# Block attention in a two-layer gated kernel: a subtraction and a score product take other places in two queues, and GpSimd takes over two small jobs

## The chip, the cores and the metric

The kernel runs on one core of one Trainium2 chip. The metric is the device time of one execution in microseconds; before the change the median of three runs is 186.9 (186.82 to 187.08). Lower is better.

## What is computed

Eight blocks of 128 rows by 256 features pass through two layers. Each layer adds a gated mixing of the context and a gated feed-forward part to its input. The change touches the second layer's attention, whose core is:

```python
q = _qdq(layernorm(x)) @ _qdq(wq).T + bq            # 16 heads of 16, int8-like rounding of inputs and weights
k, v = split(ctx @ wkv.T + bkv)
attn = softmax(q @ k.T / 4)                          # per block and head, 128 x 128
o = attn @ v
x = x + tanh(g) * (_qdq(o) @ _qdq(wp).T + bp)
def _qdq(x):
    s = max(max(abs(x), axis=-1) / 127, 1e-8)
    return clip(round(x / s), -127, 127) * s
```

Before it stand a long convolution with a router-gated low-rank product, behind it a mixture of eight experts.

## The kernel before

The kernel is written by hand, one queue per engine; the order of the instructions in each queue is the order in which the Python code issues them, and semaphores tie the queues together. Blocks are pipelined: in step s of the attention loop (s from 0 to 7) the engines work on several blocks at once. The input rounding and the query product are for block s + 2 or s + 3, the scores for block s + 1, maximum and subtraction for block s, turning, exponentials and values for block s - 1, and the output's normalisation, rounding and projection for blocks s - 2 and s - 3.

One block's way through a step, with the lines of the kernel before:

- Scores: `a_scores` (PE, L1657) multiplies 16 heads into PSUM banks 0 to 3. It overwrites the scores of the block before, so it waits for all subtractions of that block.
- Maximum: `a_max` (DVE, L1156), two halves of eight heads, written negated.
- Subtraction: `a_subtract` (DVE, L1166) for heads 0 to 11 in two instructions, and `a_last_subtract` (ACT, L781), four instructions, for heads 12 to 15.
- Turning: `a_turn(b, k)` (PE, L1671), four transposes each, k from 0 to 3, into PSUM banks 4 and 5 in turn. Turn 3 needs ACT's subtractions; each turn needs that the exponential two before it has emptied its bank.
- Exponential: `a_exp(b, k)` (ACT, L786), one for each turn.
- Values: `a_values` (PE, L1687), heads 0 to 3 and 8 to 11 after exponential 1, the others after exponential 3. Then `o_pe_` (ACT, L792) empties the bank and `o_rows` (PE, L1696) turns the result back.
- Output: `o_norm` (DVE, L1176 to L1187) has five parts: reciprocal of the sums, product, largest magnitude, scale, reciprocal of the scale. `o_round` (GpSimd, L546) rounds, `o_transpose` (PE, L1714), `o_ev_` (ACT, L811), `o_project` (PE, L1720), `o_y_` (ACT, L806), and on GpSimd `finish` (L552, L554).
- Next queries: normalised rows (`rows` on GpSimd, L535 and L538, from block 4 on), their scale (`a_quant` on DVE, L1143 to L1147), rounding `a_zq_` (ACT, L754), `a_transpose` (PE, L1618), `a_zt_` (ACT, L759), `a_project` (PE, L1624), `a_q0_` (ACT, L765), `a_q_transpose` (PE, L1631), `a_q_` (ACT, L771).

GpSimd's other work in the loop is the masked key blocks (`block_keys`, L525), `bias_rows` (L530) and, from its iteration 7 on, the normalisation's root for the experts (`late_rstd`, L559 and L561, a power). The semaphore `o_n` counts the parts of `o_norm`; `a_z` those of `a_quant`; `a_zq` and `o_qp` the rounded blocks.

Of the kernel before, what the change touches and what calls it, by code (L numbers as in the profile page):

```python
# [28 lines left out]
P = 128  # L29
# [48 lines left out]
def build(nc, x, ctxr, kern, consts, rows, cols, wff, bt, wkv, wqp, gate, w1, w3, w2, sw1, sw3, sw2, out):  # L78
    with ExitStack() as ctx:
# [3 lines left out]
        def sem(name):  # L83
            return ctx.enter_context(nc.semaphore(name))
# [28 lines left out]
        LNV = sb("LNV", [P, NB])  # L113
        EPSC = sb("EPSC", [P, 1])
        HALFM = sb("HALFM", [P, 1])
        WS = sb("WS", [P, 4])
        WR = sb("WR", [P, 4])
        SWPB = sb("SWPB", [P, DM])
# [184 lines left out]
        o_sc = sem("o_sc")  # L303
        a_zp = sem("a_zp")
        o_qp = sem("o_qp")
        y_d, x3_d = sem("y_d"), sem("x3_d")

        m_ln, m_rs, m_z, m_tr, m_zt, m_gl, m_ge, m_gt = (sem(n) for n in (
# [28 lines left out]
        WARM = 26  # L337
        FRT = 8
        AZT = 4
        ONT = 5  # L340
        LATE = 3
        MGT = 2 * GT + 4

# [76 lines left out]
        def sums(g, n):  # L420

            return PS[:, ((0, 1), (7, 6))[g][n], :]

        def expert(v):

            return v - v // (NE + 1) - 1
# [55 lines left out]
        @block.gpsimd  # L482
        def _(pool):
            nc.gpsimd.memset(ONES[:, :], 1.0).then_inc(ones_s, 1)
            nc.gpsimd.memset(HALFM[:, :], -0.5).then_inc(ones_s, 1)
            nc.gpsimd.memset(EPSC[:, :], EPS).then_inc(ones_s, 1)
            nc.gpsimd.memset(GL[:, :, :], FULL).then_inc(ones_s, 1)
# [44 lines left out]
            def rows(b):  # L532

                pool.wait_ge(a_rs, 2 * (b + 1))
                nc.gpsimd.tensor_scalar(NMR[:, b:b + 1], MV[:, b, 0:1], -1.0, None, ALU.mult).then_inc(a_zp, 1)  # L535
                pool.wait_ge(a_zq, b - 1)
                pool.wait_ge(a_zp, 2 * (b - GT) + 1)
                nc.gpsimd.tensor_scalar(AZ[:, b % 2, :], X[:, b, :], NMR[:, b:b + 1], RS[:, b:b + 1],  # L538
                                        ALU.add, ALU.mult).then_inc(a_zp, 1)

            def o_round(b):

                pool.wait_ge(o_n, ONT * (b + 1))
                if b >= 2:
                    pool.wait_ge(o_tr, b - 1)
                nc.gpsimd.tensor_scalar(OT_[:, b % 2, :], O[:, b % 2, :], OR[:, b:b + 1], ROUND_H,  # L546
                                        ALU.mult, ALU.add).then_inc(o_qp, 1)
# [71 lines left out]
            for b in range(2, NB):  # L619
                block_keys(b)  # L620
                if b == NB - 1:
                    late_rstd(0)
                if 3 <= b < NB - 1:
                    rows(b + 1)
                if b >= 6:
                    finish(b - 6)
                bias_rows(b)
                if b >= 4:
                    o_round(b - 4)
            for b in (1, 2):  # L630
                late_rstd(b)
                finish(b + 1)
                o_round(b + 3)
# [14 lines left out]
        def _(act):  # L648
# [99 lines left out]
                rstd(a_ln, 2 * (b + 1), b, b + 1, a_rs, 2 * b)  # L748

            def a_zq_(b):  # L750
                act.wait_ge(a_z, AZT * (b + 1) - max(0, b + 1 - GT))
                if b >= 2:
                    act.wait_ge(a_tr, b - 1)
                nc.scalar.activation(AT_[:, b % 2, :], AZ[:, b % 2, :], ACT.Copy, bias=ROUND_H, scale=AR[:, b:b + 1]  # L754
                                     ).then_inc(a_zq, 1)
# [36 lines left out]
                nc.scalar.copy(OTS[:, b % 2, :], PS[:, 7, :]).then_inc(o_pe, 1)  # L792

            def o_q_(b):
                act.wait_ge(o_n, ONT * (b + 1))
                if b >= 2:
                    act.wait_ge(o_tr, b - 1)
                nc.scalar.activation(OT_[:, b % 2, :], O[:, b % 2, :], ACT.Copy, bias=ROUND_H, scale=OR[:, b:b + 1]
                                     ).then_inc(o_q, 1)
# [67 lines left out]
            for s in range(NB):  # L867
                if s + 2 < NB:
                    a_zt_(s + 2)
                if s == 0:  # L870
                    a_last_subtract(0)
                    values_out(NB - 2)
                if s >= 1:
                    a_exp(s - 1, 0)
                if s + 2 < NB:
                    a_q0_(s + 2)
                if s >= 1:
                    a_exp(s - 1, 1)
                if s >= 1:
                    a_last_subtract(s)  # L880
                if s + 2 < NB:
                    a_q_(s + 2)
                if 1 <= s < NB - 4:
                    a_rstd(s + 4)
                if s >= 1:
                    a_exp(s - 1, 2)
                    a_exp(s - 1, 3)
                if s >= 3:
                    o_ev_(s - 3)
                if s + 3 < NB:  # L890
                    a_zq_(s + 3)
                if s == NB - 1:
                    m_rstd(NB - 5)
                if s >= 3:
                    o_y_(s - 3)
                if s >= 1:
                    o_pe_(s - 1)
                if s >= 5:
                    m_zt_(s - 5)
# [60 lines left out]
        def _(dve):  # L960
# [323 lines left out]
            for s in range(NB):  # L1284
                norm, new, moe, ahead = s >= 2, s + 3 < NB, s >= 4, 1 <= s < NB - 4
                if s >= 1:
                    a_max(s, 0)
                    a_max(s, 1)
                    a_subtract(s, 0)
                a_subtract(s, 1)  # L1290
                if s == 0:
                    f_out(NB - 1)
                if ahead:
                    a_stats(s + 4, 0)
                if norm:
                    o_norm(s - 2, 0)
                if ahead:
                    a_stats(s + 4, 1)
                if norm:
                    o_norm(s - 2, 1)  # L1300
                if norm:
                    o_norm(s - 2, 2)
                if s >= 5:
                    m_rows(s - 5)
                if norm:
                    o_norm(s - 2, 3)
                if new:
                    a_quant(s + 3, 0)
                if norm:
                    o_norm(s - 2, 4)  # L1310
                if new:
                    a_quant(s + 3, 1)
                if new:
                    a_quant(s + 3, 2)
                if moe:
                    m_stats(s - 4, 0)
                if new:
                    a_quant(s + 3, 3)
                if moe:
                    m_stats(s - 4, 1)  # L1320
# [113 lines left out]
        def _(pe):  # L1434
# [176 lines left out]


            def a_transpose(b):
                pe.wait_ge(a_zq, b + 1)
                chain_free(b - 2)
                for k in range(NL):
                    at = 64 * k
                    ins = TR(PS[:, a_bank(b), at:at + 64].bitcast(F16), ATH[:, b % 2, P * k:P * k + P, 0], IDH[:, :])  # L1618
                ins.then_inc(a_tr, 1)
# [58 lines left out]
            def a_values(b, k):  # L1678

                if b >= 1 and k == 0:  # L1680
                    pe.wait_ge(o_n, ONT * (b - 1) + 2)
                elif k == 0:
                    pe.wait_ge(x2, NB)
                pe.wait_ge(a_ex, 4 * b + 2 * (k % 2) + 2)
                pe.wait_ge(v_b, b + 1)
                for n in range(4):
                    ins = M(PS[VW * n:VW * n + VW, 7, P * k:P * k + P], V[:, b, 4 * k + n, :],  # L1687
                            ET[:, b % 2, place(4 * k + n), :], start=True, stop=True)
                if k == 3:
                    ins.then_inc(a_pv, 1)  # L1690
# [97 lines left out]
            for s in range(NB):  # L1788
# [16 lines left out]
                    a_q_transpose(s + 2)  # L1805
                if s >= 1:
                    a_turn(s - 1, 2)
                    a_turn(s - 1, 3)
                if s >= 1 and s + 1 < NB:
                    a_scores(s + 1)  # L1810
                if s == NB - 1:
                    m_logits(0, 0, 2)
                if s >= 3:
# [47 lines left out]
            def e_out(v):  # L1861
                g, e = divmod(v, NE + 1)
                if v < UNITS - 1:
                    pe.wait_ge(e_ht, v + 1)
                if v == 0:
                    pe.wait_ge(y_d, LATE)
                elif e == 0:
                    pe.wait_ge(o_n, ONT * (NB - 1) + 2)
                    pe.wait_ge(m_ge, NG)
                for j in range(GT):  # L1870
                    if v == UNITS - 1 and j % 2 == 0:
                        pe.wait_ge(last_ht, j // 2 + 1)
                    src = HT[:, v % 2, :] if e >= 1 else HST

                    ins = M(acc(g, j), src[:, P * j:P * j + P],  # L1875
                            W2[:, e - 1, :] if e >= 1 else SW2, start=(e == 0 and j % 2 == 0),
                            stop=(e == NE), skip_group_check=True)
                    if v == UNITS - 1 and j % 2 == 1:
                        ins.then_inc(last_acc, 1)
                if v < UNITS - 1:  # L1880
                    ins.then_inc(e_acc, 1)
# [91 lines left out]
```

## Time and profile before

| | |
|---|---|
| median of three runs | 186.9 us |
| profiled execution | 186.96 us, span 185.0 us |
| TensorE clock granted | 0.997 of full speed |
| busy over the span | PE 169.5, PEld 115.7, DVE 151.6, ACT 111.2, GpSimd 102.7 us |
| ahead of step 1 of the attention loop | 92.8 us |
| steps 1 to 7 | 47.0 us: PE 41.0, DVE 43.2, ACT 42.1, GpSimd 25.3 us busy |
| the rest | 45.2 us |

The span is the time from the first to the last instruction of the profiled execution; the time of that execution is 1.96 us longer. PE is TensorE's matmul, PEld its weight load, DVE VectorE, ACT ScalarE, POOL GpSimd. A busy time is a union of intervals, so overlapping instructions of one engine count once. A name such as L786 is a line of the kernel.

### The profile page before, as it was taken

To read this page: it belongs to the slowest core of one execution; us is meant where nothing else is said; L and a number is where in the kernel's file an instruction comes from. 1 tells how busy PE (TensorE), PEld (TensorE's weight loads), DVE (VectorE), ACT (ScalarE), POOL (GpSimd) and SP (SyncE) were. 2 spreads that over 40 slices of the span, in tenths; PEclk is the share of its full clock that TensorE was granted. 3 is DMA by queue.
4 is the path that set the end of the run, shared out by engine and by line. 5 is a ranking of instruction groups with operands and counts; after the bars stand their busy time and mean duration, and the time that the engine had idled before them with its cause. 6 is when DMAs were issued, how large, how long until landed. Compare 5 with 4: busy or idle time off the path is not lost.

```text
span 185.0 us, 3756 instructions
## 1 busy us (share of the span) xinstructions
PE 169.5 (92%) x1208; PEld 115.7 (63%) x1208; DVE 151.6 (82%) x455; ACT 111.2 (60%) x281; POOL 102.7 (55%) x177
## 2 busy tenths in 40 slices
PE   7989999998999999989768889889899899999991
PEld 7967666668565565555456666676578557656560
DVE  0799989985589989989998899999984897785663
ACT  2465044733432445764588999997799797574440
POOL 1079999996799431510295247565333569297000
PEclk9999999999999999999999999999999999999998
DMA  5979987100000000000000000000000079949943
GB/s 164 325 231 355 378 336 261 56 0 4 0 2 0 0 2 0 0 4 0 0 0 4 2 4 0 2 4 0 4 0 4 2 149 138 169 88 177 168 142 113
DMA packets 22771, 15.19 MB, mean 82 GB/s; under 512 B 17664, under 2 KB 21344, under 8 KB 22368
## 3 DMA queue, kind: packets, MB, share of 16 engines
q1 hardware_dynamic: 22112, 13.94, 29.6%
q10 hardware_dynamic: 640, 1.02, 1.5%
q8 instruction: 10, 0.16, 0.4%
q14 instruction: 9, 0.07, 0.1%
HBM read 9.68 MB, written 1.07 MB: 58 GB/s over the span
## 4 chain that ended last, share of the span: by engine, by line
PE 64%; ACT 15%; DVE 8%; DMA 5%; issue 4%; SPq 1%; DVEq 0%
PE PS L1843 9%; PE PS L1875 6%; PE PS L1473 5%; PE PS L1469 5%; PE PS L1470 5%; DMA CT<-ctxr 5%; ACT R L781 4%; ACT R L786 4%; PE PS L1574 4%; PE PS L1544 4%; PE PS L1671 4%; PE PS L1687 3%; PE PS L1508 3%; PE PS L1496 3%; PE PS L1657 2%
## 5 line engine op out<-in xcount | busy, mean ns | idle before, releaser
L1156 DVE TENSOR_REDUCE SM<-PS 128x8 f32<-128x1024 f32 x16 | 18.8, 1214 | 1.3 <-PE PS L1657 1.1
L357 POOL TENSOR_TENSOR R<-CT 128x512 f32<-128x512 f32 (+1 forms) x16 | 16.1, 1005 | 6.5 <-DMA CT<-ctxr 6.5
L573 POOL TENSOR_SCALAR R<-QT,SM 128x256 bf16<-128x256 f32 x32 | 15.9, 517 | 6.0 <-DVE SM L1235 5.7
L786 ACT ACTIVATE R<-PS 128x512 f32<-128x512 f32 x32 | 18.3, 604 | 0.8 <-PE PS L1671 0.7
L1671 PE MATMUL PS<-CON,R 128*128 128x128 f32 x128 | 18.3, 275 | 0.5 <-ACT R L786 0.5
L511 POOL TENSOR_TENSOR R<-R,ROW 128x256 f32<-128x256 f32 x8 | 5.8, 734 | 21.6 <-ACT R L723 10.9
L1357 DVE TENSOR_TENSOR R<-R,PS 128x512 bf16<-128x512 f32 (+1 forms) x17 | 11.6, 684 | 7.3 <-PE PS L1843 3.7
L582 POOL TENSOR_TENSOR R<-R 128x640 f32<-128x640 f32 (+1 forms) x12 | 15.0, 1282 | 2.8 <-DVE T_R L1081 2.8
L1671 PEld LDWEIGHTS PS<-CON,R 128*128 128x128 f32 x128 | 14.3, 140 | 2.1 <-issue 1.7
L920 ACT ACTIVATE R<-PS 128x512 f32<-128x512 f32 x17 | 10.1, 595 | 9.0 <-PE PS L1843 8.8
L1843 PE MATMUL PS<-R 128*128 128x512 bf16 x60 | 15.4, 379 | 0.0
L1166 DVE TENSOR_TENSOR R<-PS,SM 128x1024 f32<-128x1024 f32 (+1 forms) x16 | 14.5, 947 | 0.0
L1875 PE MATMUL PS<-R 128*128 128x256 bf16 (+1 forms) x80 | 13.6, 295 | 0.0
L660 ACT ACTIVATE LNV<-MV,EPSC 128x1 f32<-128x1 f32 (+1 forms) x19 | 5.6, 296 | 12.4 <-DVE MV L1075 8.9
L690 ACT CAST R<-WST 128x2048 bf16<-128x2048 f32 x3 | 5.7, 1900 | 12.1 <-DMA WST<-w 12.1
L990 DVE TENSOR_TENSOR R<-PS,QT 128x512 f32<-128x512 f32 x16 | 10.9, 683 | 2.2 <-PE PS L1473 1.6
L1473 PE MATMUL PS<-R,T_R 128*128 128x352 f32 x32 | 12.2, 462 | 0.5 <-DVE R L371 0.5
L1875 PEld LDWEIGHTS PS<-R 128*128 128x128 bf16 (+1 forms) x80 | 9.0, 117 | 5.1 <-DVE R L1357 1.9
L1469 PE MATMUL PS<-R,T_R 128*128 128x352 f32 x32 | 12.1, 459 | 0.0
L1470 PE MATMUL PS<-R,T_R 128*128 128x352 f32 x32 | 12.1, 459 | 0.0
L525 POOL TENSOR_TENSOR R<-R,CON 128x256 f32<-128x256 f32 x16 | 9.4, 612 | 3.5 <-PE PS L1657 2.1
L546 POOL TENSOR_SCALAR R<-R,SM 128x256 f32<-128x256 f32 x6 | 2.9, 477 | 15.3 <-DVE SM L1187 15.3
(172 smaller groups left out, 452.4 us busy)
## 6 DMA issues: line engine op xcount, KB each, us to landing
WST<-w SPq DMA_DIRECT2D x3, 1024.0 KB, 11.8
T_R<-lagged SPq DMA_DIRECT2D x2, 768.0 KB, 8.2
X<-x SPq DMA_DIRECT2D x2, 512.0 KB, 4.8
CT<-ctxr SPq DMA_DIRECT2D x2, 512.0 KB, 8.1
y<-X SPq DMA_DIRECT2D x8, 128.0 KB, 1.8
WQP<-wqp ACTq DMA_DIRECT2D x1, 512.0 KB, 7.3
WKV<-wkv SPq DMA_DIRECT2D x1, 512.0 KB, 10.4
R<-sw SPq DMA_DIRECT2D x3, 128.0 KB, 3.4
```

Of the source, the lines that this page charges most:

```text
L357: return eng.tensor_tensor(KV[:, h % RING, lo:hi, 0:32].rearrange("p c (i j) -> p c i j", i=4), k[:, :, 0:4].unsqueeze(3).to_broadcast([P, ...
L573: nc.gpsimd.tensor_scalar(XB[:, u % XS, j, :], MX[:, b, :], GG[:, b, e:e + 1], 1.0, ALU.mult, ALU.mult).then_inc(e_xb, 1)
L582: nc.gpsimd.tensor_tensor(pair[:, :, 0:4, at], pair[:, :, 0:4, at], pair[:, :, 4:8, at], ALU.add).then_inc(fold, 1)
L786: nc.scalar.activation(ET[:, b % 2, 4 * k:4 * k + 4, :], PS[:, 4 + k % 2, :].rearrange("p (h n) -> p h n", h=4), ACT.Exp).then_inc(a_ex, 1)
L1156: V_.tensor_reduce(MX1[:, b % 2, 8 * c:8 * c + 8], S4[:, 8 * c:8 * c + 8, :], AX.X, ALU.max, negate=True).then_inc(a_mx, 1)
L1166: V_.tensor_tensor(SS[:, a, ks, :], S4[:, ks, :], MX1[:, a, ks].unsqueeze(2).to_broadcast([P, n, P]), ALU.add).then_inc(a_sub, 1)
L1469: M(one, T[:, h, 0:P], kv[:, 0:NB], start=True, stop=True)
L1470: M(two, T[:, h, P:2 * P], kv[:, 0:NB], start=True, stop=False)
L1473: M(two, T[:, h, 0:P], kv[:, NB:2 * NB], start=False, stop=True).then_inc(conv, 1)
L1671: ins = TR(PS[:, 4 + k % 2, P * h:P * h + P], SS[:, b % 2, 4 * k + h, :], I)
L1843: ins = M(PS[:, 2 + 2 * (v % 2) + n, :], lhs, rhs, start=(k == 0), stop=(k == NL - 1))
L1875: ins = M(acc(g, j), src[:, P * j:P * j + P], W2[:, e - 1, :] if e >= 1 else SW2, start=(e == 0 and j % 2 == 0), stop=(e == NE), skip_grou ...
```

## The change

Four edits in the attention loop. First, ACT issues the four subtractions of block s directly behind `a_q0_`, ahead of exponential 1 of block s - 1, in steps 1 to 6; step 7 keeps the old place. Second, PE issues the scores of block s + 1 between turn 2 and turn 3 of block s - 1, where they followed turn 3. Third, the rounding of the inputs of blocks 4 to 7 moves from ACT (`a_zq_`) to GpSimd (`a_round`, with a semaphore of its own, `a_zqp`). Fourth, the last two parts of `o_norm` leave DVE for blocks 0 to 5: GpSimd makes the scale with a multiply and a maximum and its reciprocal with a power of minus one, inside `o_round`; `o_done` gives the new counts of `o_n`. A column of minus ones is filled at the start.

```diff
@@ gpsimd
             nc.gpsimd.memset(ONES[:, :], 1.0).then_inc(ones_s, 1)
+            nc.gpsimd.memset(MINUS[:, :], -1.0)
@@ gpsimd, rows(b)
-                pool.wait_ge(a_zq, b - 1)
+                if b < GT + 2:
+                    pool.wait_ge(a_zq, b - 1)
+                else:
+                    pool.wait_ge(a_zqp, b - GT - 1)
@@ gpsimd
+            def a_round(b):
+
+                pool.wait_ge(a_z, AZT * (b + 1) - (b + 1 - GT))
+                pool.wait_ge(a_tr, b - 1)
+                nc.gpsimd.tensor_scalar(AT_[:, b % 2, :], AZ[:, b % 2, :], AR[:, b:b + 1], ROUND_H,
+                                        ALU.mult, ALU.add).then_inc(a_zqp, 1)
+
             def o_round(b):
-                pool.wait_ge(o_n, ONT * (b + 1))
+                pool.wait_ge(o_n, o_done(b + 1, 0))
+                nc.gpsimd.tensor_scalar(OS[:, b:b + 1], OM[:, b:b + 1], 1.0 / QMAX, SMIN, ALU.mult, ALU.max
+                                        ).then_inc(o_sp, 1)
+                pool.wait_ge(o_sp, 2 * b + 1)
+                nc.gpsimd.tensor_tensor(OR[:, b:b + 1], OS[:, b:b + 1], MINUS[:, 0:1], ALU.pow).then_inc(o_sp, 1)
+                pool.wait_ge(o_sp, 2 * b + 2)
@@ gpsimd, loop over b
                 if b >= 4:
                     o_round(b - 4)
+                if 3 <= b < NB - 1:
+                    a_round(b + 1)
@@ scalar, attention loop
                 if s + 2 < NB:
                     a_q0_(s + 2)
+                if 1 <= s < NB - 1:
+                    a_last_subtract(s)
                 if s >= 1:
                     a_exp(s - 1, 1)
-                if s >= 1:
+                if s == NB - 1:
                     a_last_subtract(s)
@@
-                if s + 3 < NB:
-                    a_zq_(s + 3)
+                if s == 0:
+                    a_zq_(GT - 1)
@@ vector, attention loop
-                if norm:
-                    o_norm(s - 2, 3)
                 if new:
                     a_quant(s + 3, 0)
-                if norm:
-                    o_norm(s - 2, 4)
@@ tensor, a_transpose
-                pe.wait_ge(a_zq, b + 1)
+                if b < GT:
+                    pe.wait_ge(a_zq, b + 1)
+                else:
+                    pe.wait_ge(a_zqp, b - GT + 1)
@@ tensor, attention loop
                     a_turn(s - 1, 2)
-                    a_turn(s - 1, 3)
                 if s >= 1 and s + 1 < NB:
                     a_scores(s + 1)
+                if s >= 1:
+                    a_turn(s - 1, 3)
```

In the changed kernel lines stand some 23 to 26 further down: L759 becomes L784, L765 L790, L771 L796, L781 L806, L786 L811, L792 L817, L811 L836, L806 L831 on ACT; L1657 becomes L1683, L1671 L1697, L1687 L1713, L1714 L1740, L1720 L1746 on PE.

ACT's queue in step 4, before, from the evacuation of the transposed inputs to the end of the step (R holds the attention's buffers, SM the small columns, T_R the query, output and value copies, PS is PSUM):

```order
L759 ACTIVATE R<-PS 128x256
L786 ACTIVATE R<-PS 128x512
L765 ACTIVATE T_R<-PS,SM 128x256
L786 ACTIVATE R<-PS 128x512
L781 ACTIVATE R<-PS,SM 128x128 x4
L771 ACTIVATE R<-PS,COL,WS 128x128 x2
L786 ACTIVATE R<-PS 128x512 x2
L811 ACTIVATE R<-PS 128x256
L754 ACTIVATE R<-R,SM 128x256
L806 ACTIVATE T_R<-PS,SM 128x256
L792 COPY T_R<-PS 128x512
```

The same step in the changed kernel:

```order
L784 ACTIVATE R<-PS 128x256
L811 ACTIVATE R<-PS 128x512
L790 ACTIVATE T_R<-PS,SM 128x256
L806 ACTIVATE R<-PS,SM 128x128 x4
L811 ACTIVATE R<-PS 128x512
L796 ACTIVATE R<-PS,COL,WS 128x128 x2
L811 ACTIVATE R<-PS 128x512 x2
L836 ACTIVATE R<-PS 128x256
L831 ACTIVATE T_R<-PS,SM 128x256
L817 COPY T_R<-PS 128x512
```

The four subtractions stand ahead of exponential 1 now, and the rounding L754 is gone; the rest keeps its order.

PE's queue in step 4, before, from turn 1 to the last values (the eight turns are turn 2 and turn 3):

```order
L1671 MATMUL PS<-CON,R 128x128 x4
L1631 MATMUL PS<-CON,T_R 128x128 x2
L1671 MATMUL PS<-CON,R 128x128 x8
L1657 MATMUL PS<-R 128x256 x8
L1714 MATMUL PS<-IDH,R 128x128 x2
L1687 MATMUL PS<-R 32x128 x8
L1720 MATMUL PS<-R 128x256 x2
L1687 MATMUL PS<-R 32x128 x8
```

The same stretch in the changed kernel:

```order
L1697 MATMUL PS<-CON,R 128x128 x4
L1657 MATMUL PS<-CON,T_R 128x128 x2
L1697 MATMUL PS<-CON,R 128x128 x4
L1683 MATMUL PS<-R 128x256 x8
L1697 MATMUL PS<-CON,R 128x128 x4
L1740 MATMUL PS<-IDH,R 128x128 x2
L1713 MATMUL PS<-R 32x128 x8
L1746 MATMUL PS<-R 128x256 x2
L1713 MATMUL PS<-R 32x128 x8
```

Turn 3 stands behind the scores, and the output's transpose and the values follow it.

## Rows read from the trace of the kernel before

**Rows 1.** Stretches 4, 5: length, busy PE, PEld, DVE, ACT, POOL, clock, DMA, GB/s.

```profile
113.78:120.45 6.67, 6.16 (x82) 4.42 (x79) 6.43 (x15) 6.35 (x17) 4.54 (x8) 1.00 0.01 1
120.45:127.51 7.06, 6.47 (x84) 4.70 (x81) 6.65 (x13) 6.21 (x17) 4.28 (x8) 1.00 0.01 2
```

**Rows 2.** Chain of waits, step 4: start us, us, engine and line.

```profile
115.93 0.47 issue
116.40 1.15 ACT R L781 x4
```

**Rows 3.** Timeline of ACT, step 4: start us, us, line, operation [idle before].

```profile
114.59 0.38 ACT L759 ACTIVATE R<-PS 128x256 bf16<-128x256 f16 x1
...
115.47 0.47 ACT L765 ACTIVATE T_R<-PS,SM 128x256 f32<-128x256 f32 x1
115.90 0.60 ACT L786 ACTIVATE R<-PS 128x512 f32<-128x512 f32 x1
...
118.56 0.65 ACT L786 ACTIVATE R<-PS 128x512 f32<-128x512 f32 x1
...
119.08 0.40 ACT L811 ACTIVATE R<-PS 128x256 bf16<-128x256 f16 x1
119.36 0.52 ACT L754 ACTIVATE R<-R,SM 128x256 f32<-128x256 f32 x1
119.98 0.47 ACT L806 ACTIVATE T_R<-PS,SM 128x256 f32<-128x256 f32 x1
```

**Rows 4.** Timeline of PE, step 4.

```profile
117.68 1.15 PE L1657 MATMUL PS<-R 32*128 32x256 f32 x16 [0.37 <-ACT R L781]
118.76 0.29 PE L1714 MATMUL PS<-IDH,R 128*128 128x128 f16 x2
...
119.55 0.39 PE L1720 MATMUL PS<-R 128*128 128x256 bf16 x2
...
120.94 0.28 PE L1618 MATMUL PS<-IDH,R 128*128 128x128 f16 x2
```

**Rows 5.** Timeline of PE, step 2: the last values.

```profile
106.14 0.64 PE L1687 MATMUL PS<-R 128*32 128x128 f32 x16 [0.28 <-ACT R L786]
```

**Rows 6.** Timeline of DVE, step 4 and the start of step 5.

```profile
112.42 2.34 DVE L1156 TENSOR_REDUCE SM<-PS 128x8 f32<-128x1024 f32 x2
114.67 1.81 DVE L1166 TENSOR_TENSOR R<-PS,SM 128x1024 f32<-128x1024 f32 x2
...
117.60 0.15 DVE L1185 TENSOR_SCALAR SM<-SM 128x1 f32<-128x1 f32 x1
...
117.96 0.42 DVE L1143 TENSOR_REDUCE SM<-R 128x1 f32<-128x256 f32 x1
...
119.04 2.32 DVE L1156 TENSOR_REDUCE SM<-PS 128x8 f32<-128x1024 f32 x2
```

**Rows 7.** Timeline of PE, step 6: turns 1 and 2.

```profile
128.39 1.13 PE L1671 MATMUL PS<-CON,R 128*128 128x128 f32 x8
```

**Rows 8.** Timeline of ACT, step 6.

```profile
128.15 0.60 ACT L786 ACTIVATE R<-PS 128x512 f32<-128x512 f32 x1
129.02 0.60 ACT L786 ACTIVATE R<-PS 128x512 f32<-128x512 f32 x1 [0.28 <-PE PS L1671]
...
132.20 0.38 ACT L811 ACTIVATE R<-PS 128x256 bf16<-128x256 f16 x1 [0.57 <-PE PS L1714]
```

**Rows 9.** Timeline of ACT, step 2: subtractions and the last exponential.

```profile
102.86 1.14 ACT L781 ACTIVATE R<-PS,SM 128x128 f32<-128x128 f32 x4
...
105.50 0.59 ACT L786 ACTIVATE R<-PS 128x512 f32<-128x512 f32 x1
```

**Rows 10.** Timeline of GpSimd, step 4.

```profile
118.12 0.47 POOL L546 TENSOR_SCALAR R<-R,SM 128x256 f32<-128x256 f32 x1 [1.54 <-DVE SM L1187]
...
120.21 0.22 POOL L559 TENSOR_SCALAR LNV<-MV 128x1 f32<-128x1 f32 x1
120.51 0.58 POOL L561 TENSOR_TENSOR RS<-LNV,HALFM 128x1 f32<-128x1 f32 x1
```

More of the change, by code:

```diff
@@ L115, in build @@
         HALFM = sb("HALFM", [P, 1])
+        MINUS = sb("MINUS", [P, 1])
         WS = sb("WS", [P, 4])
@@ L305, in build @@
         o_qp = sem("o_qp")
+        o_sp = sem("o_sp")
+        a_zqp = sem("a_zqp")
         y_d, x3_d = sem("y_d"), sem("x3_d")
@@ L339, in build @@
         AZT = 4
-        ONT = 5
+        LAST_O = NB - 2
         LATE = 3
@@ L422, in sums, with o_done @@
             return PS[:, ((0, 1), (7, 6))[g][n], :]
+        def o_done(b, k):
+            return 3 * min(b, LAST_O) + 5 * max(b - LAST_O, 0) + k
         def expert(v):
@@ L750, in a_zq_ @@
             def a_zq_(b):
-                act.wait_ge(a_z, AZT * (b + 1) - max(0, b + 1 - GT))
+                act.wait_ge(a_z, AZT * (b + 1))
                 if b >= 2:
@@ L794, in o_q_ @@
             def o_q_(b):
-                act.wait_ge(o_n, ONT * (b + 1))
+                act.wait_ge(o_n, o_done(b + 1, 0))
                 if b >= 2:
@@ L1680, in a_values @@
                 if b >= 1 and k == 0:
-                    pe.wait_ge(o_n, ONT * (b - 1) + 2)
+                    pe.wait_ge(o_n, o_done(b - 1, 2))
                 elif k == 0:
@@ L1867, in e_out @@
                 elif e == 0:
-                    pe.wait_ge(o_n, ONT * (NB - 1) + 2)
+                    pe.wait_ge(o_n, o_done(NB - 1, 2))
                     pe.wait_ge(m_ge, NG)
```

## The prediction

> **What bounds the kernel now.** I first read the busy times by step [rows 1] to see which engine could be the limit of the attention loop, the stretch from 92.8 to 139.8 us in which all of the edits act. Three engines are close to full there: in step 4 (113.78 to 120.45, 6.67 us, counted from turn 0 of the block before on PE) DVE is busy for 6.43, ACT for 6.35, PE for 6.16, GpSimd for 4.54. A busy share does not say which one the step waits for, so I went on to the chain of waits [rows 2]. It runs through the last subtraction on ACT (L781, 1.15), then the scores (L1657), and ahead of the subtraction it shows 0.47 of "issue": that is the second exponential, 115.90 to 116.40, which the subtraction waits behind without needing it. Read by itself this row promises half a microsecond a step.
>
> The timeline of ACT [rows 3] says otherwise. From the evacuation at 114.59 to the end of the fourth exponential at 119.21 ACT never stands: L759, exponential 0, L765, exponential 1, four subtractions, two L771, exponentials 2 and 3, one behind the other with no idle time noted. After that comes L811 at 119.08, and PE takes its result at 119.55 for the output projection, then the last values, then turn 0 of the next block at 120.45 [rows 1, 4]. So the step is a loop: ACT's queue from L759 to L811, then PE's short tail back to the next L759. The scores are a side branch of it. They start at 117.68 after 0.37 of idle PE [rows 4], and what PE does behind them (output transpose at 118.76, values, projection at 119.55) arrives 0.07 after L811 has ended (119.48): the side branch ties with the main one and does not lead it. Step 2 shows this openly: there PE, which has already waited for the subtraction ahead of its scores, waits 0.28 more for the last exponential, at 106.14 [rows 5]. Scores that start sooner would lengthen the second wait by as much as they shorten the first.
>
> **The change part by part.** Everything is reckoned against the profiled execution: 186.96 us, span 185.0, 1.96 around it. The median of the runs is 186.9, so the two agree and a difference carries over.
>
> *The subtraction ahead of exponential 1, steps 1 to 6.* ACT's queue holds the same instructions in another order, so L759 to exponential 3 costs the same sum. In step 4 the subtraction starts after L765, at 115.90 in place of 116.40. Its data are there: the second maximum ends at 114.76 (112.42 plus 2.34), the DVE subtraction at 116.48 [rows 6], before the scores would start. So the subtraction ends 0.50 earlier, at 117.04, and the scores follow by the 0.14 of the old pair (117.54 to 117.68), at 117.18. Gain on the loop: nothing, since ACT is the loop. Exponential 1 goes to 116.90, and L771 stays where it was.
>
> *Scores ahead of turn 3.* This is the edit that costs. Exponential 3 needs turn 3, and turn 3 now stands on PE behind the scores. The trace of before has no turn behind scores; the nearest row is the transpose at 118.76, 1.08 after the scores' start [rows 4]. From the start of a turn to the exponential that waits for it, step 6 has 128.39 to 129.02, 0.63 [rows 7, 8]. So in step 4: 117.18 + 1.08 + 0.63 = 118.89, while ACT's slot for exponential 3 is 118.56 [rows 3]. ACT now stands for **0.33 us**, and L811, the projection, the last values and the next turn 0 all come 0.33 later. PE does not hide it: behind turn 3 it reaches the projection at 118.26 + 0.49 (a turn, 120.45 to 120.94) + 0.79 (118.76 to 119.55) = 119.54 [rows 1, 4] and waits for L811 there. Step 5 has the same queue and the same wait: another 0.33. Bounds for one of them: 0.15 if the turn overlaps the scores more than the transpose did, 0.55 if it starts only at the scores' full end (1.15) and the clean-up costs a semaphore more, which is the 0.14 above.
>
> Steps 1 to 3 have the two small instructions of the normalisation (L660, L663) between L771 and exponential 2. In step 2 the subtraction ends at 104.00 now [rows 9], 103.50 then; plus 0.14, 1.08 and 0.63 gives 105.35, and exponential 3 has its slot at 105.50. It fits by 0.15, so nothing is lost or won in these three.
>
> Step 6 has no L759, L765 and L771. Today ACT waits there for turn 1 (0.28) and later for the output transpose (0.57, L811 at 132.20) [rows 8]. With the new order the subtraction runs behind exponential 0 (128.15 plus a slot of 0.50) from 128.65 to 129.79; scores at 129.93, turn 3 at 131.01, exponential 3 at 131.64, L811 0.52 behind it (118.56 to 119.08) at 132.16: **-0.04**. Step 7 keeps the old order.
>
> *Rounding the inputs on GpSimd (blocks 4 to 7) and no longer on ACT.* The ACT instruction is L754, 0.52 at 119.36 [rows 3]. It lies behind L811, in the stretch in which ACT waits for PE's tail anyway: the next one, L806, starts only when the projection has ended. Removing it gives nothing. On GpSimd it costs about what L546 costs, 0.47 [rows 10], and the transpose that waits for it (L1618, a step later) stands at 120.94 in step 4 [rows 4]; the rounded rows of block 7 would be there by about 118.8, behind the output's rounding of L546 at 118.12.
>
> *The output's scale on GpSimd.* DVE loses L1185 and L1187: from 117.60 to 117.96, 0.36 a step [rows 6], in six steps. The DVE is not on the loop (its maximum is done more than a microsecond before the subtraction may start), so this is room and not time: 0. GpSimd gains a small multiply (like 0.22 at 120.21) and a power (like 0.58 at 120.51), with 0.30 from the one's start to the other's [rows 10]; the rounded output is ready 0.30 + 0.58 + 0.47 = 1.35 us and three semaphores after DVE's reduction. Its reader, the output transpose, runs a whole step later. GpSimd's load in step 4 [rows 1] becomes 4.54 + 0.47 + 0.22 + 0.58 = 5.8 of 6.7 us: full, but with its readers over a microsecond away. The new one-column constant at the start of the program is one short fill while the first load is under way: 0.
>
> **Sum:** 0.33 + 0.33 - 0.04 = +0.62. What follows the loop (the gates, the experts) hangs on step 7's PE order and moves with it. 186.9 + 0.6 = **187.5 us**.
>
> **The rivals.**
>
> *Faster: the subtraction and DVE were the limit after all.* For it speaks the chain [rows 2] with its 0.47 before the subtraction, and that DVE starts the maximum of block 5 at 119.04 with no idle time ahead of it [rows 6]. Then the step shortens by what DVE loses, 0.36, in steps 2 to 6: 5 x 0.36 = 1.8, and 185.1 us. It decides if PE's wait for the last exponential (0.28 in step 2) is a product of today's order and not of ACT's queue. Against it: ACT without a gap from 114.59 to 119.21. Chance 0.17. The Trainium skill, page "Perfetto Trace Analysis", section "Identifying the Most-Contended Engine", says that the engine with the highest occupancy is the one to relieve first; by that rule DVE, with 6.43 of 6.67, is the one, and this rival is what would happen. The trace speaks against the rule here: DVE runs full and yet early.
>
> *No change: the wait at exponential 3 is hidden.* ACT gives up L754's 0.52 a step, and in four steps it has more room than the 0.33 it loses. If the turn follows the scores closely and the tail catches up in that room, -0.04 is left: 186.9. Against it: L754's room lies behind L811 and the wait lies ahead of it. Chance 0.25.
>
> *Slower by more: GpSimd becomes the limit.* It has 5.8 us of work in a step, in one queue, with the power's result awaited by the rounding and the block keys behind that. If these take a third longer than their rows, it needs 7.7 a step, its input rounding arrives behind PE's transpose in steps 3 to 5, and three steps lose up to 0.7 on top: 189. Against it: its wait for DVE is 1.54 long in step 4 today [rows 10]. Chance 0.05.
>
> That the change would not do what it says I leave out: the queues show the new orders directly.
>
> **How the numbers follow.** My forecast (two waits of 0.33, each between 0.15 and 0.55, so +0.26 to +1.06; at the upper bound steps 1 to 3 would each lose 0.07 too, 0.22 less their 0.15, which makes +1.3) has 0.53, and its own range is 187.1 to 188.2. The range that should hold 8 in 10 takes in no change with some 0.7 below it, for a part of DVE's gain, and leaves out the full DVE gain and the GpSimd case: 186.2 to 188.3. A measurement of this kernel can tell about 0.2%, 0.37 us, from no change. Slower: 0.48 of the forecast and the 0.05 of GpSimd, 0.53. Same: the other 0.05 of the forecast and 0.21 of the hidden wait, 0.26. Faster: DVE's 0.17 and 0.04 of the hidden wait, 0.21.
>
> **What would show it.** Right: in steps 4 and 5 a wait of about 0.3 on ACT ahead of exponential 3, released by PE's turn; steps 1 to 3 and 6 as long as before; steps 4 and 5 at 7.0 and 7.4, from 6.67 and 7.06 [rows 1]; scores half a microsecond nearer to the step's start; DVE waiting for scores in every step. Wrong: steps under 6.4 us, or no wait at exponential 3, or PE's input transpose waiting for GpSimd.

## The result and the profile after

The changed kernel takes 187.26 us in the median (187.02 to 187.53, 17 runs), the kernel before 186.88 on the same chip (17 runs): ratio 1.0021, 95% interval 1.0015 to 1.0028. It is slower by 0.38 us. That is the size that the prediction called just about measurable; with this many runs the interval leaves no room for "no change". The profiled execution is 187.42 with a span of 185.6 (before 186.96 and 185.0).

The first row of the page, busy time of each engine over the span:

```profile
PE 170.2 (92%) x1208; PEld 116.0 (63%) x1208; DVE 150.6 (81%) x443; ACT 109.3 (59%) x277; POOL 109.4 (59%) x194
```

ACT and DVE have less to do than before (111.2 and 151.6), GpSimd more (102.7), as the edits say, and the kernel is slower. Where the time went shows in the steps, each counted from PE's turn 0 to the next turn 0:

| step | 1 | 2 | 3 | 4 | 5 | 6 | 7 |
|---|---|---|---|---|---|---|---|
| before, us | 7.44 | 6.47 | 7.07 | 6.67 | 7.06 | 6.45 | 5.84 |
| after, us | 7.39 | 6.39 | 6.99 | 6.93 | 7.33 | 6.40 | 5.98 |
| difference, from unrounded starts | -0.05 | -0.08 | -0.08 | +0.26 | +0.27 | -0.05 | +0.15 |

The seven differences make +0.42. With the loop starting 0.10 later (92.91, from 92.81) that is +0.52 of the span's +0.54; but the loop's start lies anywhere between 92.66 and 92.92 in the profiled executions of this case, so the 0.10 need not belong to the change. Steps 4 and 5 lose, as forecast; all else is small.

Busy time by step, steps 4 and 5, with the columns of [rows 1] (window, length, then PE, PEld, DVE, ACT, POOL):

```profile
113.68:120.61 6.93, 6.27 (x82) 4.46 (x78) 6.06 (x13) 5.98 (x16) 6.24 (x12) 1.00 0.00 1
120.61:127.94 7.33, 6.59 (x84) 4.73 (x81) 6.33 (x11) 6.25 (x17) 4.69 (x10) 1.00 0.01 2
```

In step 4 DVE goes from 6.43 busy to 6.06 and ACT from 6.35 to 5.98, and the step from 6.67 to 6.93: both were relieved, and neither relief became time.

ACT's timeline in step 4, against [rows 3]:

```profile
114.49 0.38 ACT L784 ACTIVATE R<-PS 128x256 bf16<-128x256 f16 x1
...
115.37 0.47 ACT L790 ACTIVATE T_R<-PS,SM 128x256 f32<-128x256 f32 x1
115.74 1.13 ACT L806 ACTIVATE R<-PS,SM 128x128 f32<-128x128 f32 x4
116.74 0.62 ACT L811 ACTIVATE R<-PS 128x512 f32<-128x512 f32 x1
117.22 0.84 ACT L796 ACTIVATE R<-PS,COL,WS 128x128 f32<-128x128 f32 x2
117.90 0.65 ACT L811 ACTIVATE R<-PS 128x512 f32<-128x512 f32 x1
118.79 0.60 ACT L811 ACTIVATE R<-PS 128x512 f32<-128x512 f32 x1 [0.24 <-PE PS L1697]
119.29 0.38 ACT L836 ACTIVATE R<-PS 128x256 bf16<-128x256 f16 x1
```

The four subtractions (now L806) stand ahead of exponential 1 (L811), and exponential 3 waits for PE's turn (L1697). The noted 0.24 counts from the end of exponential 2; the delay is larger, since neighbours on ACT start before the one ahead has ended. From the evacuation of the input transpose (L784, before L759) to exponential 3 it is 118.79 - 114.49 = 4.30, before 118.56 - 114.59 = 3.97: 0.33.

PE in step 4, against [rows 4]:

```profile
117.02 1.15 PE L1683 MATMUL PS<-R 32*128 32x256 f32 x16 [0.25 <-ACT R L806]
118.10 0.66 PE L1697 MATMUL PS<-CON,R 128*128 128x128 f32 x4
...
119.72 0.39 PE L1746 MATMUL PS<-R 128*128 128x256 bf16 x2 [0.28 <-ACT R L836]
...
120.61 0.66 PE L1697 MATMUL PS<-CON,R 128*128 128x128 f32 x4
```

The scores start 3.34 after the step's start (before 117.68 - 113.78 = 3.90), so the first two edits do bring them forward by more than half a microsecond. Turn 3 follows 1.08 behind them. And PE, which used to wait 0.37 ahead of the scores and nowhere behind them, now waits 0.25 there and 0.28 more at the output projection for ACT: part of the wait has moved down the queue.

The chain of waits says the same as a path. In step 4 of the kernel before it went, behind the subtraction of [rows 2], along PE alone, from the scores through the values to the next turn 0, without exponential 3:

```profile
117.68 1.15 PE PS L1657 x16
...
119.05 0.57 PE PS L1687 x16
...
119.95 0.57 PE PS L1687 x16
120.52 0.59 PE PS L1671 x4
```

In the changed kernel it leaves PE behind turn 3 and comes back at the projection:

```profile
117.02 1.15 PE PS L1683 x16
118.17 0.60 PE PS L1697 x4
...
118.79 0.60 ACT R L811
119.39 0.28 ACT R L836
...
119.72 0.39 PE PS L1746 x2
```

Scores, turn 3, exponential 3, evacuation, projection: before, the scores' branch and exponential 3's ran beside each other and ended almost together; now they stand one behind the other.

From the page's costliest groups, with the idle time ahead of each group at the end:

```profile
L1183 DVE TENSOR_REDUCE SM<-PS 128x8 f32<-128x1024 f32 x16 | 18.9, 1218 | 2.7 <-PE PS L1683 2.4
L811 ACT ACTIVATE R<-PS 128x512 f32<-128x512 f32 x32 | 18.7, 605 | 2.2 <-PE PS L1697 2.0
```

ACT now stands 2.0 us ahead of exponentials for a turn (0.7 before), and DVE 2.4 us ahead of its maximum for scores (1.1 before). Only 0.24 in each of steps 4 and 5 is the forecast wait; 0.94 of ACT's 2.0 falls in step 6, where no step time is lost.

### The profile page after: what moved, and what is told of

It is laid out like the page before. It is cut to its first block, busy times and chain, and to the rows that moved or that the text cites. A ratio compares the mean times of both kernels' runs of the same rounds, so it can differ in the third digit from the quotient of the medians.

```text
span 185.6 us, 3754 instructions
## 1 busy us (share of the span) xinstructions
PE 170.2 (92%) x1208; PEld 116.0 (63%) x1208; DVE 150.6 (81%) x443; ACT 109.3 (59%) x277; POOL 109.4 (59%) x194
## 3 DMA queue, kind: packets, MB, share of 16 engines
HBM read 9.68 MB, written 1.07 MB: 58 GB/s over the span
## 4 chain that ended last, share of the span: by engine, by line
PE 63%; ACT 16%; DVE 8%; DMA 5%; issue 4%; SPq 1%; DVEq 0%
PE PS L1870 9%; PE PS L1902 6%; ACT R L811 5%; PE PS L1496 5%; PE PS L1492 5%; PE PS L1493 5%; DMA CT<-ctxr 5%; ACT R L806 4%; PE PS L1597 4%; PE PS L1697 4%; PE PS L1567 4%; PE PS L1531 3%; PE PS L1519 3%; PE PS L1683 2%; PE PS L1614 2%
## 5 line engine op out<-in xcount | busy, mean ns | idle before, releaser
L811 ACT ACTIVATE R<-PS 128x512 f32<-128x512 f32 x32 | 18.7, 605 | 2.2 <-PE PS L1697 2.0
L1697 PE MATMUL PS<-CON,R 128*128 128x128 f32 x128 | 19.5, 278 | 0.3 <-ACT R L811 0.2
L1697 PEld LDWEIGHTS PS<-CON,R 128*128 128x128 f32 x128 | 14.2, 140 | 3.8 <-issue 3.5
L1463 PE MATMUL PS<-ONES 128*128 128x128 f32 x60 | 10.3, 341 | 1.0 <-POOL ONES L491 1.0
L1683 PE MATMUL PS<-R 32*128 32x256 f32 x112 | 8.0, 398 | 3.0 <-ACT R L806 1.7
```

The costliest lines, as they stand in the source:

```text
L811: nc.scalar.activation(ET[:, b % 2, 4 * k:4 * k + 4, :], PS[:, 4 + k % 2, :].rearrange("p (h n) -> p h n", h=4), ACT.Exp).then_inc(a_ex, 1)
L1697: ins = TR(PS[:, 4 + k % 2, P * h:P * h + P], SS[:, b % 2, 4 * k + h, :], I)
```

## The experiments

The theory: in the loop of steps 4 and 5 ACT's queue leads; turn 3 behind the scores makes exponential 3 late; what DVE and ACT give to GpSimd is not on the loop. The rivals: the loss comes from GpSimd's longer queue, or from the subtraction's new place. The step lengths below are counted as above. All ratios are to the kernel before on the same chip (186.73 us for the first eight kernels below, 186.88 for the ninth and the tenth, 186.85 for the last two).

### GpSimd's two jobs alone

The changed kernel with both old queue orders:

```diff
@@ ACT, step s
-                if 1 <= s < NB - 1:
-                    a_last_subtract(s)
                 if s >= 1:
                     a_exp(s - 1, 1)
-                if s == NB - 1:
+                if s >= 1:
                     a_last_subtract(s)
@@ PE, step s
                     a_turn(s - 1, 2)
+                    a_turn(s - 1, 3)
                 if s >= 1 and s + 1 < NB:
                     a_scores(s + 1)
-                if s >= 1:
-                    a_turn(s - 1, 3)
```

> GpSimd's two jobs alone, both queue orders as before. If ACT's queue is the loop: no change against before, within 0.15 us (186.9), steps 1 to 7 as long as before. If DVE or ACT's total load were the limit: the 0.36 us that DVE loses in each of steps 2 to 6 shows, some 1.8 us faster. If GpSimd becomes the limit: slower than before by more than 0.4 us, with PE's input transpose waiting for GpSimd.

Measured: 186.70 us, ratio 0.9998 (0.9989 to 1.0007), and every one of the seven steps equal to before within 0.01 us. So GpSimd's work costs nothing, and the 0.36 a step that DVE gives up and the 0.5 that ACT gives up bring nothing. DVE's maximum and ACT's next evacuation in step 4:

```profile
118.93 2.35 DVE L1181 TENSOR_REDUCE SM<-PS 128x8 f32<-128x1024 f32 x2 [0.85 <-PE PS L1681]
```

```profile
120.03 0.47 ACT L831 ACTIVATE T_R<-PS,SM 128x256 f32<-128x256 f32 x1 [0.49 <-PE PS L1744]
```

The time taken off both engines has turned into waiting, 0.85 for the scores and 0.49 for the projection, in the places that the prediction had named.

### The subtraction's new place alone

The changed kernel with turn 3 back ahead of the scores (the PE half of the diff above).

> The changed kernel with turn 3 put back ahead of the scores; the subtraction stays ahead of exponential 1. If the loss came from the scores' place in PE's queue: it is gone, as before or better (186.9 or less). If it came from the subtraction's place, since turn 3 must then wait for the later exponential 1 and the scores behind it: as slow as the changed kernel within 0.2 us (187.1 to 187.4), with PE reaching the output projection in steps 4 and 5 at the same moment as in the changed kernel.

Measured: 187.94, ratio 1.0069 (1.0055 to 1.0083): a miss. Undoing the edit that I held to be the costly one made the kernel slower still. Steps 4 and 5 are 7.15 and 7.55, each 0.48 or 0.49 over before; steps 3 and 6 are 0.08 and 0.17 longer, the others as before. PE and ACT in step 4 (step start 113.72):

```profile
117.55 0.63 PE L1697 MATMUL PS<-CON,R 128*128 128x128 f32 x4 [0.74 <-ACT R L811]
118.10 1.15 PE L1683 MATMUL PS<-R 32*128 32x256 f32 x16
119.18 0.28 PE L1740 MATMUL PS<-IDH,R 128*128 128x128 f16 x2
```

```profile
119.51 0.39 ACT L836 ACTIVATE R<-PS 128x256 bf16<-128x256 f16 x1 [0.43 <-PE PS L1740]
```

Turn 3 needs the bank that exponential 1 empties. Exponential 1 now runs behind the subtraction, so turn 3 waits for it 0.74, and the scores wait behind turn 3: they start 4.38 into the step, not 3.90. The output transpose stands behind the scores, and ACT waits for that. This is the side branch that tied with the loop before; 0.48 later it leads, and the step grows by 0.48. My expectation had left out that PE's queue holds the scores behind a turn which needs exponential 1.

### The scores' new place alone

The kernel before with only the PE edit.

> The kernel before with the scores ahead of turn 3 and nothing else. If exponential 3 waits for subtraction, scores and turn 3 in a row (0.14 + 1.08 + 0.63 us behind the subtraction's end, at 119.39 in step 4 where its slot is 118.56): 0.83 us lost in each of steps 4, 5 and 6 and 0.35 in each of steps 1 to 3, +3.5 us, about 190.4. If the tail hides the wait: within 1 us of before.

Measured: 190.48, ratio 1.0198 (1.0184 to 1.0212), as expected. Each of steps 1 to 6 loses, 0.42 in the first three (0.35 expected) and 0.82 or 0.83 in the next three. PE and ACT in step 4:

```profile
118.92 1.15 PE L1657 MATMUL PS<-R 32*128 32x256 f32 x16 [0.81 <-ACT R L781]
119.99 0.66 PE L1671 MATMUL PS<-CON,R 128*128 128x128 f32 x4
```

```profile
120.69 0.60 ACT L786 ACTIVATE R<-PS 128x512 f32<-128x512 f32 x1 [0.73 <-PE PS L1671]
```

Here the scores stand and wait for a subtraction in its old, late place, and turn 3 waits behind them; the turn follows by 1.07 and exponential 3 by 0.70 more, the two distances of the changed kernel. So neither order can be had alone: together they lose in two steps, each alone it loses more.

### The old orders in steps 4 and 5 only

The changed kernel with `EARLY = (1, 2, 3, 6)`: ACT and PE keep their new orders where `s in EARLY`, and the old ones elsewhere.

> The changed kernel with both old orders in steps 4 and 5 alone. If the two waits of 0.24 us at exponential 3 are the loss: steps 4 and 5 go back to 6.7 and 7.06 us, and the time is 0.5 us under the changed kernel and 0.1 us under the kernel before (186.7 to 186.8), since steps 1, 2, 3 and 6 keep the 0.04 to 0.08 us that each of them was shorter. If the loss lies elsewhere (GpSimd, the start, step 7): it stays at 187.1 or more.

Measured: 186.61, ratio 0.9989 (0.998 to 0.9997). Steps 4 and 5 are back at 6.67 and 7.06, all others as in the changed kernel within 0.02. The loss lies in these two steps and in these two orders.

### ACT really stands there: an idle copy in the gap

The changed kernel with one more instruction on ACT, a 128x128 copy of ones into a scratch tile between exponentials 2 and 3 (the tile's allocation is left out):

```diff
+                    if s in (4, 5):
+                        nc.scalar.copy(SCR[:, s - 4, :], ONES[:, :])
```

> The changed kernel with one idle copy (128 x 128, a slot of some 0.25 to 0.30 us on ACT) ahead of exponential 3 in steps 4 and 5; its result is read by nobody. If ACT stands there for turn 3, the copy fills the wait: 187.2 to 187.4, no more than 0.1 us above the changed kernel. If the steps are long because ACT has too much to do: 0.5 us above the changed kernel, 187.8.

Measured: 187.08, ratio 1.0017 (1.0008 to 1.0026), steps 4 and 5 at 6.94 and 7.33, as in the changed kernel. ACT in step 4:

```profile
117.73 0.65 ACT L812 ACTIVATE R<-PS 128x512 f32<-128x512 f32 x1
118.21 0.35 ACT L916 COPY SCR<-ONES 128x128 f32<-128x128 f32 x1
118.61 0.60 ACT L812 ACTIVATE R<-PS 128x512 f32<-128x512 f32 x1
```

0.35 us of useless work fits and costs nothing, and the wait's note is gone: ACT now looks busy from end to end while the step is as long. A queue without idle marks is therefore not yet the bound, which matters for the reading of [rows 3]. That ACT bound step 4 before rests on the next run, not on its full look.

### Less work on ACT: three heads instead of four

If ACT's queue is the loop, a shorter subtraction must pay. Old orders, GpSimd's two jobs, and from block 1 on DVE subtracts 13 heads and ACT 3. DVE does its second half first, and ACT waits for that half, so that the two don't read that bank at once (reading it from both was not tried). The cut leaves out the order of DVE's two halves and the semaphore counts that follow from the new split.

```diff
+        def on_act(b):
+            return 4 if b == 0 else 3
@@ ACT, a_last_subtract
+                if b >= 1:
+                    act.wait_ge(a_sub, 2 * b + 1)
-                for j in range(4):
+                for j in range(4 - on_act(b), 4):
@@ DVE, a_subtract
-                a, ks = b % 2, slice(8 * c, (8, 12)[c])
+                a, ks = b % 2, slice(8 * c, (8, 16 - on_act(b))[c])
```

> Both old queue orders, GpSimd's two jobs as in the change, and in blocks 1 to 7 DVE subtracts 13 heads where it subtracted 12 and ACT three in place of four (DVE does the second half first, since two engines may not read one PSUM bank at once). If ACT's queue between the evacuation and exponential 3 is the loop: 0.25 us less in each of steps 1 to 7, 1.2 to 1.8 us under before, about 185.2. If the scores' branch on PE or DVE is the limit: less than 0.5 us.

Measured: 185.42, ratio 0.9933 (0.992 to 0.9947). Steps 1 to 6 are 7.18, 6.22, 6.82, 6.41, 6.81 and 6.20: each 0.25 or 0.26 shorter than before. ACT in step 4:

```profile
115.61 0.88 ACT L816 ACTIVATE R<-PS,SM 128x128 f32<-128x128 f32 x3
116.36 0.83 ACT L804 ACTIVATE R<-PS,COL,WS 128x128 f32<-128x128 f32 x2
117.05 1.11 ACT L821 ACTIVATE R<-PS 128x512 f32<-128x512 f32 x2
```

Three subtractions take 0.88, four took 1.15 [rows 2]; what leaves ACT's queue leaves the step. The subtractions stand ahead of exponential 3 and ahead of the scores, so this shows that the loop runs through ACT's queue up to them, and not which of the two branches behind them ends last. The run also swaps DVE's two halves; no run has that swap alone, but six steps that lose the length of one subtraction each speak for ACT. This is the lowest median of all kernels here, 1.31 under the kernel before.

### Two heads, and the same without GpSimd's jobs

The same with `2` for `3`, and then that split in the kernel before, where ACT still rounds the inputs and DVE still makes the output's scale. The first:

> The same with 14 heads on DVE and two on ACT. If ACT's queue is the loop: 0.5 us less a step, up to 3.4 us, as far as DVE keeps up (its own work in steps 2 and 3 then takes about 6.4 us): 183.7 to 184.6. If DVE becomes the limit at once: no better than three heads on ACT.

Measured: 185.76, ratio 0.9951 (0.9938 to 0.9963): the hoped-for 183.7 to 184.6 was missed, and the second case came true, no better than three heads. Step 2 is 0.51 shorter than before, as forecast, but from step 3 on DVE starts each step's maximum without a noted wait:

```profile
111.64 2.34 DVE L1191 TENSOR_REDUCE SM<-PS 128x8 f32<-128x1024 f32 x2
```

DVE has become the limit in these steps. The second:

> The kernel before (DVE makes the output's scale, ACT rounds the inputs) with 14 heads on DVE and two on ACT. If the output's scale on GpSimd is worth nothing in any order: as fast as the kernel with GpSimd's jobs and two heads. If it is worth something only where DVE is the limit: slower than that by up to 0.36 us in each of steps 2 to 4, 0.5 to 1.2 us in all.

Measured: 188.24, ratio 1.0083 (1.0069 to 1.0096): 2.48 us behind the same split with GpSimd's jobs, twice the top of what I had expected. PE waits for DVE's subtraction in step 3:

```profile
110.81 1.15 PE L1668 MATMUL PS<-R 32*128 32x256 f32 x16 [0.81 <-DVE R L1176]
```

So the two jobs that are worth nothing in the kernel before are worth 2.5 us where DVE leads. How much of it comes from DVE's job and how much from ACT's was not separated.

### Three heads without GpSimd's jobs

> The kernel before with three heads on ACT and 13 on DVE, and none of GpSimd's new jobs. If GpSimd's jobs gain nothing unless DVE is the limit, and DVE with 13 heads is near it (its own work about 6.3 us plus the 0.36 of the output's scale against steps of 6.2 to 6.8): 0.3 to 1.2 us slower than three heads with GpSimd's jobs, 185.7 to 186.6. If DVE still has room: the same 185.4.

Measured: 187.40, ratio 1.0028 (1.0018 to 1.0038), and so 1.0028 - 0.9933, nearly one per cent or 1.8 us, behind the same split with them; I had expected at most 1.2. Steps 1 and 2 are equal to those with the jobs (7.17 and 6.21), from step 3 on each is longer, step 7 most (6.62 for 5.75). PE in step 4 waits for DVE:

```profile
117.14 1.15 PE L1668 MATMUL PS<-R 32*128 32x256 f32 x16 [0.26 <-DVE R L1176]
```

DVE's backlog grows and is paid later. Counted from the loop's start, its maximum behind step 2 starts 0.82 later than with the jobs, the one behind step 3 1.32, the one behind step 4 1.69. In each of these additions 0.36 is the output's scale, whose sum over the steps I had priced too low. But 0.46 of the first 0.82 is a stand of DVE between the scale and its reciprocal, in step 2 alone, for which the profile names no other engine:

```profile
104.88 0.17 DVE L1197 RECIPROCAL SM<-SM 128x1 f32<-128x1 f32 x1 [0.46 <-DVE SM L1195]
```

The kernel before has the same 0.46 at the same place (L1187), where DVE had room for it, and so has the kernel before with two heads; with these two instructions on GpSimd it does not occur. Its cause was not tested.

### Three heads with the new orders

Do the new orders help where ACT's subtraction is shorter? First in steps 1, 2, 3 and 6:

> Three heads on ACT, GpSimd's jobs, and in steps 1, 2, 3 and 6 the change's two queue orders. If those orders bring 0.04 to 0.08 us a step there, as in the changed kernel: 0.1 to 0.3 us under the old orders with three heads, 185.1 to 185.3. If with three heads ACT's subtraction now waits for DVE or turn 3 comes too late for exponential 3: equal or slower, 185.4 or more.

Measured: 186.21, ratio 0.9963 (0.9949 to 0.9976), worse than three heads with the old orders. Against the old orders, steps 2 and 3 gain 0.08 each, steps 1 and 6 lose 0.33 and 0.43. ACT in step 6:

```profile
130.80 0.60 ACT L822 ACTIVATE R<-PS 128x512 f32<-128x512 f32 x1 [1.21 <-PE PS L1709]
```

Then in steps 2 and 3 alone:

> Three heads on ACT, GpSimd's jobs, and the change's two orders in steps 2 and 3 alone. Those two steps were 0.08 and 0.09 us shorter with the new orders there, steps 1 and 6 were 0.33 and 0.43 longer. If the steps add up: 0.1 to 0.2 us under three heads with the old orders, 185.2 to 185.3, and the fastest so far. If the orders in two steps disturb the steps behind them: 185.4 or more.

Measured: 185.60, ratio 0.994 (0.9928 to 0.9953): a miss, the hoped-for gain is not there. Step 2 is 6.22 as without, step 3 is 6.96 for 6.82. PE in step 3:

```profile
109.69 1.15 PE L1695 MATMUL PS<-R 32*128 32x256 f32 x16 [0.28 <-DVE R L1204]
110.77 0.66 PE L1709 MATMUL PS<-CON,R 128*128 128x128 f32 x4
```

In step 3 the scores wait for DVE's subtraction of 13 heads, and with the new order turn 3 waits behind them. The profiled execution took 185.92, one of the two longer of its five (the other three took 185.59 to 185.60), so how much of step 3's 0.14 belongs to the order is open. That the small gains of steps 2 and 3 are had only behind a slow step 1, as in the kernel above, is a guess that no run tested.

### The old orders in steps 4, 5 and 6

This is for the 0.15 us that step 7 lost, though its own orders are as before on ACT: does step 6's order cause it? The changed kernel with `EARLY = (1, 2, 3)`.

> The changed kernel with both old orders in steps 4, 5 and 6. If the 0.15 us by which step 7 is longer in the changed kernel (5.98 against 5.84) comes from the new order in step 6: it is gone, step 6 back to 6.45, step 7 to 5.84, and the time 0.1 us under that with old orders in 4 and 5 alone. If it does not come from there: step 7 stays at 5.98 and the time is 186.6 to 186.7.

Measured: 186.74, ratio 0.9995 (0.9986 to 1.0004). Step 6 is back at 6.45, step 7 stays at 5.98. So step 6 is not the cause. The 0.15 is there in this kernel, in the changed one, in the one with old orders in steps 4 and 5 and in the one with the copy, and not with GpSimd's jobs alone or the subtraction's place alone. The traces show where it arises. Before, PE goes from its last two transposes to turn 0 of the next block in 0.34:

```profile
139.46 0.41 PE L1773 MATMUL PS<-CON,QT 128*128 128x128 f32 x2
139.80 1.06 PE L1671 MATMUL PS<-CON,R 128*128 128x128 f32 x8
```

In the changed kernel it takes 0.50:

```profile
139.83 0.41 PE L1799 MATMUL PS<-CON,QT 128*128 128x128 f32 x2
140.33 0.84 PE L1697 MATMUL PS<-CON,R 128*128 128x128 f32 x6
```

Up to these transposes step 7 is as long in both (5.49). DVE's subtraction and ACT's exponential that turn 0 needs had ended 4.7 and 1.9 us ahead of it, so the 0.15 is no wait for their work. Its cause stays open.

## Why the prediction was right, and where its steps were off

- **The direction and its mechanism.** Right, with the size too large: +0.38 us in the medians and +0.46 in the profiled executions, for +0.62. Exponential 3 waits for a turn behind the scores, in steps 4 and 5 and in no step before them. What stands behind it was shown from both sides: with the old orders in these two steps alone the loss is gone, and 0.35 us of filler in the wait costs nothing.
- **The size of the wait, "ACT now stands for 0.33 us".** The delay of exponential 3 is 0.33 to the hundredth, but by two errors that cancel: the turn follows the scores by 1.08 as taken, the exponential follows the turn by 0.69 and not 0.63, and the subtraction starts 0.06 sooner than forecast.
- **The term of the sum, 0.33 a step.** This one was too large: the steps grew by 0.26 and 0.27. Behind the wait, in step 4, the way from exponential 3 to the next turn 0 is shorter by 0.07: exponential 3 to L836 takes 0.50 (before 0.52), L836 to the projection 0.43 (before 119.55 - 119.08 = 0.47), the projection to turn 0 0.89 (before 0.90). In the 0.47 is the tie that the prediction itself had found: PE's side branch held the projection to 0.07 behind L811's end; now that this branch is early, 0.05 pass. The evacuation itself is 0.02 shorter (0.38 for 0.40). I used the tie to show that the scores don't lead and did not credit it when they moved; it is worth 0.02 of the 0.07. It also had the wrong side: PE can start 0.05 behind L836's end, before it started 0.07 behind L811's, so the scores' branch came last by 0.02, which is the way that the chain of waits took. The conclusion stands, since earlier scores alone could have gained no more than some 0.02 in step 4, an estimate from these two distances. Why the two ACT pieces are 0.02 shorter each was not tested.
- **Steps 1 to 3, "nothing is lost or won".** No wait came, but each is 0.05 to 0.08 shorter. On ACT in step 4 the instruction behind the query evacuation starts 0.37 later when it is a subtraction (115.37 to 115.74) and 0.43 later when it is an exponential (115.47 to 115.90 in [rows 3]), and the pair behind exponential 1 follows in 0.48 (116.74 to 117.22) for its 0.50 before. That is 0.08 from L765 to the pair (1.93 before, 1.85 after), so "the same sum" in another order is not exact to 0.1 us.
- **Step 6, -0.04.** It is -0.05. Exponential 3 there was forecast at 131.64 and a start of the evacuation at 132.16; the profile has the exponential at

```profile
132.13 0.60 ACT L811 ACTIVATE R<-PS 128x512 f32<-128x512 f32 x1 [0.94 <-PE PS L1697]
```

  which in a program that by then runs 0.43 later (0.10 - 0.20 + 0.53) is 131.70 on the old clock: right within 0.06.
- **Step 7, left out of the sum.** It lost 0.15, unexplained. Of the +0.54 of the span, 0.53 is the two forecast waits (0.66 in the forecast), and the small terms (0.10 at the start, 0.15 in step 7, -0.25 in steps 1 to 3 and 6) happen to cancel. That the total came so near to the two waits is luck.
- **GpSimd, 0.** Right in time (186.70 against 186.73 with these jobs alone). The load of step 4 is 6.24 of 6.93 us for the forecast 5.8 of 6.7, but the surplus is work that came sooner and falls into step 4 instead of 5: over both steps GpSimd is busy for 2.11 more than before, and the rows, with no input left to round in step 5, give 2.07. The output's scale, its power, the output's rounding and the inputs' rounding in step 4:

```profile
116.67 0.22 POOL L562 TENSOR_SCALAR SM<-SM 128x1 f32<-128x1 f32 x1
116.98 0.57 POOL L565 TENSOR_TENSOR SM<-SM,MINUS 128x1 f32<-128x1 f32 x1
117.65 0.48 POOL L569 TENSOR_SCALAR R<-R,SM 128x256 f32<-128x256 f32 x1
118.10 0.48 POOL L556 TENSOR_SCALAR R<-R,SM 128x256 f32<-128x256 f32 x1
```

  Each costs what [rows 10] said, and PE's next input transpose, at 121.11, notes no wait.
- **The rival "the subtraction and DVE were the limit".** Refuted. DVE waits for the scores in the changed kernel (the profile notes it in five of the seven steps, where the forecast had every step):

```profile
118.22 2.36 DVE L1183 TENSOR_REDUCE SM<-PS 128x8 f32<-128x1024 f32 x2 [0.77 <-PE PS L1683]
```

  The rule of the Trainium skill named beside that rival ("Perfetto Trace Analysis", section "Identifying the Most-Contended Engine"), to relieve the engine with the highest occupancy first, does not lead to a gain in the kernel before: DVE has the highest, 6.43 of 6.67 us, and 0.36 us a step off DVE together with 0.5 off ACT left the time at 186.70 against 186.73. With a shorter ACT queue the same two jobs together are worth 1.8 to 2.5 us.
- **The rival "hidden wait".** Refuted by the same run of GpSimd's jobs alone: the room of L754 lies behind the projection, where ACT now waits 0.49, and exponential 3's wait lies ahead of it.

## What to carry to other kernels

When several engines are near full, find the loop and its side branches, and note the ties: an edit that delays one of them is absorbed as far as another had arrived later still (here that was 0.02 of the 0.33, and the step took up 0.07 in all). Two orders that hand work to each other, here ACT's subtraction and PE's scores, must be costed as a pair and each by itself, with every instruction queued behind the waiting one: alone they lost 1.2 and 3.75 us, together 0.4. And before calling relief of a full engine worthless, shorten the engine that leads: the same two jobs were worth nothing, and then 1.8 us.

## What the runs showed of the hardware that was not expected

- The spacing of neighbours on ACT depends on the pair: 0.37 or 0.43 us behind the same 128x256 evacuation, 0.48 or 0.50 behind the same 128x512 exponential.
- A queue with no idle note may still hold slack: ACT took a 128x128 copy of 0.35 us between two exponentials with no change in the step (6.94 against 6.93).
